# Four-layer convolution block on one core: second convolution from row-shifted halves, as 32-column matmuls on four column strips

## The reference, cut to what matters

```python
# x: (64, 16, 128, 128); _gn: group normalisation over 8 groups of 2 channels
x = x + newton_schulz(_gn(x), 5)            # layer 0: 128x128 inverses, 5 iterations
x = x + conv3x3_int8(_gn(x), W1, s1, b1)    # layer 1: activations rounded to int8 steps
x = x + _L2_conv_ref(_gn(x), filter_w)      # layer 2
x = x + circular_conv3x3(_gn(x), W3)        # layer 3, circular padding

def _L2_conv_ref(x, filter_w):              # filter_w: (16, 16, 5)
    kernel = filter_w[..., :, None] * jnp.eye(5)
    return conv_general_dilated(x, kernel, padding=((2, 2), (2, 2)), ...)
```

## Time and profile before

| | before |
|---|---|
| median of 3 runs | 4286.94 us (4285.88 to 4287.16) |
| profiled execution: span | 4285.7 us |
| PE busy | 4194.6 us (98%) |
| DVE busy | 3444.2 us (80%) |
| ACT busy | 2072.5 us (48%) |
| POOL busy | 2407.9 us (56%) |
| matmuls of layers 1 to 3, taps (L1392) | 6912 recorded, 1661.6 us |
| matmuls of layers 1 to 3, neighbour rows (L1399) | 1792 recorded, 515.6 us |
| HBM | 135.22 MB read, 134.22 MB written |

### The profile page before, as it was taken

How to read it: one execution, slowest core, us unless ns; L and a number is a source line. 1 busy time by engine, 2 the same in 40 slices (tenths; PEclk the granted TensorE clock), 3 DMA queues, 4 the chain that set the end, 5 groups by cost and what they waited for, 6 DMA issues and landing times. The chain is left out here.

```text
span 4285.7 us, 81705 instructions
## 1 busy us (share of the span) xinstructions
PE 4194.6 (98%) x30409; PEld 3108.7 (73%) x30409; DVE 3444.2 (80%) x7393; ACT 2072.5 (48%) x4296; POOL 2407.9 (56%) x3149
## 2 busy tenths in 40 slices
PE   7999999999999999999996999999999999999998
PEld 7999999999999999999992444444444444444443
DVE  6888888888888888888876787878787888888784
ACT  5776777777777777777761222222222222222221
POOL 6888888888888888888871222222222222222221
PEclk9999999999999999999997999999999999999999
DMA  2221222222222222222214555555555555555553
GB/s 69 64 62 55 65 65 60 60 60 60 60 66 65 60 63 68 60 60 60 60 41 97 133 137 134 137 133 137 134 138 134 138 134 138 134 138 134 138 134 84
DMA packets 333657, 404.28 MB, mean 94 GB/s; under 512 B 23088, under 2 KB 286032, under 8 KB 316880
## 3 DMA queue, kind: packets, MB, share of 16 engines
q1 hardware_dynamic: 308688, 334.25, 30.8%
q10 hardware_dynamic: 24576, 64.79, 5.6%
HBM read 135.22 MB, written 134.22 MB: 63 GB/s over the span
## 5 line engine op out<-in xcount | busy, mean ns | idle before, releaser
L1392 PE MATMUL bank<-xn,wt 128*128 128x512 f16 (+1 forms) x6912 | 1661.6, 381 | 19.9 <-issue 10.7
L1164 POOL TENSOR_TENSOR xn<-F,xn 128x512 f16<-128x512 f32 x512 | 541.6, 1090 | 1453.2 <-ACT xn L1202 1453.2
L1392 PEld LDWEIGHTS bank<-xn,wt 128*128 128x128 f16 (+1 forms) x6912 | 672.9, 100 | 805.0 <-issue 21.9
L463 ACT ACTIVATE P<-bank 128x512 f32<-128x512 f32 x1024 | 606.8, 608 | 264.0 <-PE bank L962 154.5
L1266 DVE SCALAR_TENSOR_TENSOR x<-bank,wu,x 128x512 f32<-128x512 f32 x512 | 382.4, 747 | 313.7 <-PE bank L1399 306.6
L1202 ACT ACTIVATE xn<-F 128x2048 f16<-128x2048 f32 x128 | 244.9, 1913 | 603.3 <-DVE F L1322 603.3
L1399 PE MATMUL bank<-xh,wth 96*128 96x512 f16 (+1 forms) x1792 | 515.6, 380 | 12.1 <-DMA xh<-xn 12.1
L313 POOL TENSOR_TENSOR W<-W 128x512 f16<-128x512 f32 x256 | 290.3, 1166 | 145.7 <-ACT W L489 145.7
L1277 DVE BATCH_NORM_STATS2 bs<-x 128x6 f32<-128x512 f32 x512 | 355.6, 695 | 17.7
L569 DVE BATCH_NORM_STATS2 st<-X 128x6 f32<-128x256 f32 x1024 | 351.5, 411 | 5.8 <-DMA X<-in_x 5.7
L1399 PEld LDWEIGHTS bank<-xh,wth 96*128 96x128 f16 (+1 forms) x1792 | 174.2, 97 | 232.6 <-DMA xh<-xn 15.7
(11 more groups left out here) (129 smaller groups left out, 7619.3 us busy)
## 6 DMA issues: line engine op xcount, KB each, us to landing
X<-in_x SPq DMA_DIRECT2D x64, 1024.0 KB, 4.8
x_scratch<-X SPq DMA_DIRECT2D x64, 1024.0 KB, 5.6
X<-x_scratch SPq DMA_DIRECT2D x64, 1024.0 KB, 8.8
out<-x SPq DMA_DIRECT2D x64, 1024.0 KB, 3.9
xh<-xn SPq DMA_DIRECT2D x384, 131.8 KB, 4.5
xh<-xn ACTq DMA_DIRECT2D x384, 131.8 KB, 5.4
xh<-xn SPq DMA_DIRECT2D x192, 65.9 KB, 3.2
xh<-xn ACTq DMA_DIRECT2D x192, 65.9 KB, 2.7
```

The source lines that it names most:

```text
L463: nc.scalar.activation(into[:, 4 * q:4 * q + 4, :], banks[q][:, :].rearrange("p (m w) -> p m w", m=4), ACT.Copy).then_inc(sb, 1)
L1164: ins = nc.gpsimd.tensor_tensor(padded(xn[l][odd], 1)[:, a + 1:a + 5, L:L + H], F[l][:, a:a + 4, :], padded(xn[l][odd], 0)[:, a + 1:a + 5, ...
L1392: nc.tensor.matmul(bank, wt[l][:, a, k, :], v, start=(k == a == b == 0), stop=False)
```

## The change

Layer 2 is computed from another copy of its input and with other matmuls.

- **Copy.** `xk` (two buffers, [128, 2, SFLAT] float16) holds both halves of `xn[2]`, with row r of every band moved right by 7 - r elements (`skew_row`). It takes eight DMAs an image of 16 partitions x 2 halves x 4216 bytes: rows 0, 2, 4, 6 on SP's queue, rows 1, 3, 5, 7 on ACT's. They replace the six of `halos` for layer 2, which have the same size. In `xk` the diagonal stands upright: all inputs of output row o lie at one column offset, 7 - o.
- **Matmuls.** The taps are summed into one matrix (`wsum`). For each bank (`diagonals`), each product and each e in {0, 1}, four matmuls of 32 weight columns write the four 32-partition quarters q of the bank, each reading all 128 partitions of `xk` at the offset of output row 2q + e; the weights of the other row of the quarter are zero. For the neighbouring bands there are two more of 32 columns for each e, on quarters 0 and 3. That is 24 + 12 = 36 matmuls a bank, in the order of quarters 0 1 2 3, 0 1 2 3, 0 3, 0 3 for each product. The built program gives them tile positions (0, 0), (0, 32), (0, 64), (0, 96) and tile size 128x32.
- **Waits.** PE waits for all eight DMAs ahead of the first matmul of layer 2; before it waited for the six ahead of the 16th. `mean(2, s)` stands behind bank 1 (before: inside it), `var(2, s)` behind bank 2 (before: behind bank 1).
- **Once.** Weights: a sum over the taps, three more memsets, the copies and subtractions in two pieces each, six small weight DMAs in place of one. POOL zeroes both `xk` at the start of the second stage, 128x4784 float16 each, and the DMAs wait for that.

```diff
+            def skew_row(eng, r, odd):
+                at, to = PW + L, PW + L + SK - r
+                eng.dma_start(xk[odd][C * r:C * r + C, :, to:to + RUN],
+                              xn[2][odd][C * r:C * r + C, :, at:at + RUN]).then_inc(skewed[odd], 16)
...
+                    def skew(n, odd):
+                        sp.wait_ge(normed[2], n + 1)
+                        sp.wait_ge(xk_zeroed, 2)
+                        for r in range(0, RB, 2):
+                            skew_row(sp, r, odd)
...
                         if there(s):
-                            halos(2, s, odd)
+                            skew(s, odd)
...
+                    for n in range(2):
+                        nc.gpsimd.memset(xk[n][:, :, :], 0.0).then_inc(xk_zeroed, 1)
...
                             act.wait_ge(normed[2], s + 1)
-                            halos(2, s, odd)
+                            act.wait_ge(xk_zeroed, 2)
+                            for r in range(1, RB, 2):
+                                skew_row(act, r, odd)
...
+                    def diagonals(s, n, h, odd, u):
+                        bank = banks[(BPI + u) % B_RING]
+                        if u == 0:
+                            pe.wait_ge(skewed[odd], 16 * RB * (h + 1))
+                        bank_free(s, 2, u)
+                        def rows(b, o, back):
+                            at = (4 * u + 1) * PW + L + SK - o + back * (PW + RB)
+                            return xk[odd][:, b, at:at + 4 * PW].rearrange("p (j w) -> p j w", w=PW)[:, :, 0:H]
+                        for a, b in [(0, 0), (0, 1), (1, 0)]:
+                            for e in range(2):
+                                for q in range(4):
+                                    nc.tensor.matmul(bank[32 * q:32 * q + 32, :], wt[2][:, a, e, 32 * q:32 * q + 32],
+                                                     rows(b, 2 * q + e, 0), start=(a == b == e == 0),
+                                                     stop=(a == e == 1 and q in (1, 2)))
+                            for e in range(2):
+                                for q, back in ((0, -1), (3, 1)):
+                                    ins = nc.tensor.matmul(bank[32 * q:32 * q + 32, :], wth[2][:, a, e, 32 * q:32 * q + 32],
+                                                           rows(b, 2 * q + e, back), start=False, stop=(a == e == 1))
+                        ins.then_inc(conv_ps[2], 1)
...
                             for u in range(BPI):
-                                conv(2, s, s - 1, h + odd - 1, 1 - odd, u,
-                                     (lambda: mean(2, s)) if u == 1 and there(s) else None)
+                                diagonals(s, s - 1, h + odd - 1, 1 - odd, u)
                                 if there(s) and u == 1:
+                                    mean(2, s)
+                                if there(s) and u == 2:
                                     var(2, s)
```

More of the change, by code:

```diff
@@ L262, in _ @@
                     load(2, 0, 2)
-                    for l, body, rows in ((1, w1, w1h), (2, w2, w2h), (3, w3, w3h)):
+                    for l, body in ((1, w1), (2, w2), (3, w3)):
                         sp.dma_start(wf[l][:, :, :], body).then_inc(w_loaded, 16)
+                    for l, rows in ((1, w1h), (3, w3h)):
                         sp.dma_start(whf[l][:, :], rows).then_inc(w_loaded, 16)
+                    sp.wait_ge(ones_set, 4)
+                    for k, (row, _, o) in enumerate(HALO2):
+                        r = row % RB
+                        sp.dma_start(whf[2][C * r:C * r + C, C * o:C * o + C],
+                                     w2h[C * k:C * k + C, C * o:C * o + C]).then_inc(w_loaded, 16)
                     for i in range(A_FIRST):
@@ L476, in upper_weights @@
                         if l == 1:
-                            act.wait_ge(w_loaded, 16 * 6)
+                            act.wait_ge(w_loaded, 16 * W_PIECES)
                         else:
-                            act.wait_ge(w_chain, 6 * (l - 1))
-                        nc.scalar.activation(wt[l][:, 0, :, :], wf[l][:, :, :], ACT.Copy).then_inc(w_high, 1)
-                        nc.scalar.activation(wth[l][:, 0, :], whf[l][:, :], ACT.Copy).then_inc(w_high, 1)
+                            act.wait_ge(w_chain, (7, 13)[l - 2])
+                        if l == 2:
+                            act.wait_ge(ones_set, 6)
+                            for to, of in ((wt[2], wsum), (wth[2], whf[2])):
+                                for e in range(2):
+                                    ins = nc.scalar.activation(by_row(to[:, 0, e, :], e), by_row(of[:, :], e), ACT.Copy)
+                                ins.then_inc(w_high, 1)
+                        else:
+                            nc.scalar.activation(wt[l][:, 0, :, :], wf[l][:, :, :], ACT.Copy).then_inc(w_high, 1)
+                            nc.scalar.activation(wth[l][:, 0, :], whf[l][:, :], ACT.Copy).then_inc(w_high, 1)
                     def upper_w(n, q):
@@ L702, in weight_scale @@
                         w = wtop[l]
-                        link = Link(dve, w_chain, 6 * (l - 2) + 2)
+                        link = Link(dve, w_chain, (0, 7)[l - 2] + 2)
                         dve.wait_ge(w_top_all, l - 1)
                         link.done(nc.vector.tensor_copy(w["s"][:, :], banks[7][:, H - 4 + l:H - 3 + l]))
+                        if l == 2:
+                            link.done(nc.vector.tensor_reduce(wsum[:, :], wf[2][:, :, :].rearrange("p k m -> p m k"), AX.X,
+                                                              ALU.add))
                         link.wait()
@@ L1071, in conv_net @@
             T = sb("T", [H, NJ, H])
-            xh = [None] + [[sb(f"xh{l}_{n}", [6 * C, parts[l], NJ * PW], kinds[l]) for n in range(2)] for l in (1, 2, 3)]
+            xh = [None] + [None if l == 2 else [sb(f"xh{l}_{n}", [6 * C, parts[l], NJ * PW], kinds[l]) for n in range(2)]
+                           for l in (1, 2, 3)]
+            xk = [sb(f"xk{n}", [H, 2, SFLAT], f16) for n in range(2)]
             F = [None, None] + [sb(f"F{l}", [H, NJ, H]) for l in (2, 3)]
@@ L1133, in load @@
                     def load(n, h, odd):
-                        stand(sp, evac[1], BPI * (n - 1), w_loaded, 16 * 6)
+                        stand(sp, evac[1], BPI * (n - 1), w_loaded, 16 * W_PIECES)
                         sp.dma_start(xs[1][odd][:, :, :],
```

54 lines of the change are left out of this document (40 added, 14 removed).

## The result

The changed kernel takes 4314.72 us (median of 4 runs, 4311.02 to 4316.35); the kernel before takes 4287.05 (4 runs, 4285.88 to 4288.18). The ratio is 1.0064, with a 95% interval of 1.005 to 1.0078: slower by 0.64%, three times what can be told from no change. The forecast was 4249, faster. The profiled execution of the changed kernel has a span of 4312.0 us and a time of 4313.79.

What follows compares the result with a forecast made beforehand. PE bound the kernel at 30.52 us a step; about 62 steps x (30.52 - 29.9) = 38 us off 4285.7 gives 4248, and a median 1.2 higher 4249. Its own range was 4215 to 4278, with rivals 4165 to 4400.

Steps and rivals of the forecast that it cites:

- Loop 1: Copy landing, layer 2's banks and statistics, DVE, ACT, POOL, next copy: longest loop, 29.6 us a step (28.5 to 31.1).
- PE saves 5.2 us a step: Layer 2's matmuls on PE: strips side by side, 12 turns a bank, take PE from 30.52 to 25.3 us a step.
- serial strips: Rival in layer 2: strips run one after another, 15.7 us a step more on PE, 5290 us; chance 0.07.
- imperfect overlap: Rival in layer 2: one unhidden weight load of 0.056 us each turn, loop through the copy 31.6, 4355 us; chance 0.10.
- I take 8.8: Layer 2's copy: the last of eight halves lands 8.8 us after the start, between bounds of 7.7 and 10.3.
- late copy at 11.5: Rival at layer 2's copy: it lands at 11.5 us, +112 us, 4400; chance of a late copy 0.17.
- no fast one: Rival at layer 2's copy: it lands as fast as six halves did, 7.7 us, giving 4169 us; chance 0.12.
- I price the six of a step at nothing: Six changes of the array's tiling a step on PE, claimed to cost 0 from an earlier trace.
- This rival: Tiling changes around layer 2's statistics drain the array: three at 0.28 us, period 30.7 with the clock, 4298 us; chance 0.02.
- The clock: PE's clock falls after its new pauses: 0.3 us a step on average, period 29.9; rival of most steps falling, 0.12.
- Loops 2 and 3: Loops through the root (28.6 us) and through the third layer's mean (28.3 us), both shorter than the longest loop.
- Once ... in all 0: One-time costs: memsets 2 (0 to 8), first layer 2 +3, last layer 2 -5, weights' pieces 0; in all 0 us.

Runs made afterwards that it cites:

- the ninth experiment: Kernel before, with the second layer's mean and variance each as four matmuls of 32 weight columns, its other matmuls 128 wide: 4292.83 us, ratio 1.0014.

## Why the prediction was wrong

The mechanism was right and the sign was not: the forecast had a gain of 0.6 us a step in hand, and its terms together were off by 0.81. Two terms of Loop 1 were mis-sized by about as much each, the changes of tiling (0, measured +0.41) and the copy (8.8, measured +0.38 to the first strip); neither alone uses up the 0.6, and both together turn the sign.

- **PE saves 5.2 us a step: right.** Strips beside one another, a bank in 12 turns, 2.61 us. The rivals of serial strips and of imperfect overlap (a bank over 2.9 us) didn't come about. The Trainium skill ("TensorE: Matmul & The Clock Gate", section Part 3, Packing small matmuls) has loads overlap only between different row groups, and gives a factor of 2.38 for three column strips. Here four column strips on the same 128 rows load and run four to a turn, and a bank's 36 strips take 2.61 us, where 36 matmuls one after another at 0.217 would take 7.8: a factor of 3.0, so the measurement decides against both.
- **Loop 1 through the copy becomes the period: right**, and shown from both sides, by six rows (1.77 us a step for 1.78 us of copy) and by the waits alone in the kernel before (+1.5 us a step). All links that were taken over from the earlier trace rows came out as read: 3.85 (3.83), 2.34, 1.99, 4.26.
- **"I take 8.8" for the copy: mis-sized, it takes 9.14.** The issues were right; a half on ACT's queue lands 5.7 us after its issue with eight in flight, not 5.4. The late copy at 11.5 didn't come about, and no fast one either. +0.38 with the 0.04 to the first matmul.
- **"I price the six of a step at nothing": the step that failed**, since it put a term at zero that had a size. From the first strip to DVE's use of the variance it takes 8.80 us, not 8.4. The 0.11 us of the earlier trace rows stood for one small matmul among wide ones, which the ninth experiment roughly bears out, but around a wide matmul among packed strips there are 0.31 us on either side. This rival got 0.02, because a row of another situation was held against it. The Trainium skill ("TensorEngine Tiling (Array Packing)", section Key Properties) says that switching the mode drains the engine. The trace here agrees in that the statistic starts 0.31 us behind the last strip, where the kernel before has 0.21 between its last wide matmul and the variance, though a weight load that can't run ahead would look the same. The rival's period, 30.7, is the measured one, but in part by chance: it had 0.8 for the draining and the shorter copy, where the runs show 0.4 and the longer one.
- **The clock: right in size.** 0.3 us a step was put in; the mean step is 0.28 above the median and 0.22 above the steps without a fall. Filling the pauses shows that 0.1 may be nearer.
- **Loops 2 and 3: not binding, as forecast.** The root starts 4.36 us after the first issue (4.56), the first residual 6.92 after it (6.98).
- **"Once ... in all 0": wrong, it was +15.** The memsets cost 7.7 (I took 2 of 0 to 8), the first copy and the clock behind it 7.4 and 2.8 (I took 3), the end gained 2.5 (I took 5).

In sum: 0.81 x 58 = +47 in the steady steps and +15 once, against a forecast of -38, come out at +24 to +26. The chance of 0.40 for slower was mostly given to mechanisms that didn't occur; what did occur was two small terms of one loop in the same direction, and the forecast's own range, 4215 to 4278, had no room for both. Where the margin (0.6 us in 30.5) is smaller than the sum of the unmeasured terms' bounds, the sign isn't known.

## What to carry to other kernels

When an edit makes the bound engine faster, write down the chain from its output back to its input, with every DMA latency that the old order hid, and count the new period from there; then move what closes that loop (here mean and variance) ahead in the same edit. The same strips lost 28 us with the mean behind bank 1 and won 76 with it inside, with the statistics in the strips' tiling and only the edges cleared. A memset of a whole buffer in idle time of POOL isn't free while DVE works; clear only what nothing else writes.

## What the runs showed that I had not expected

- A wide matmul between packed strips costs 0.62 us from the last turn ahead of it to the first behind it, where a plain spacing is 0.217 and wide among wide is 0.36. The same sum in four strips in the strips' own tiling removes this (8.80 to 8.21 us on the loop).
- Two operations of DVE, 1.34 and 1.23 us alone, took 5.12 and 5.07 beside POOL's memset of 128x4784 float16 elements x2, and 1.37 and 1.33 beside the small ones.
- Two more halves in the copy (132 KB each) cost 1.78 us of landing, while shifts by single elements cost 0.2.
- Of 57 steps 25 have a fall of the clock, most behind a pause of some 2.5 us. With the pauses filled the clock stays up, but that gains almost nothing: of the 30.4 us of the loop through the copy only the 8.8 from the first strip to the variance are PE's, the rest is DVE, ACT, POOL and DMA.
